# Selecting 32 of 48 keys by dropping the 16 smallest in place of keeping the 32 largest

## The reference

```python
scores = jnp.einsum('bhqd,bhkd->bhqk', q, k) / math.sqrt(D_HEAD)
scores = jnp.where(causal, neg_inf, scores)
vals, idx = jax.lax.top_k(scores, K_S)               # K_S = 32
masked = jnp.put_along_axis(jnp.full_like(scores, -jnp.inf), idx, vals, axis=-1, inplace=False)
attn = jax.nn.softmax(masked, axis=-1)
out = jnp.einsum('bhqk,bhkd->bhqd', attn, v)
...
x = _layernorm(x + attention(x))
x = _layernorm(x + experts(x, ctx_512, itok))
x = _layernorm(x + ffn(x))
```

## Time and profile before

| what | value |
|---|---|
| median of three runs | 606.18 us (605.2 to 607.4) |
| the profiled execution | 605.08 us |
| its span | 603.3 us |
| mean granted clock of TensorE | 0.952 |
| PE busy | 527.5 us (87%) |
| DVE busy | 472.6 us (78%) |
| ACT busy | 385.9 us (64%) |
| POOL busy | 344.5 us (57%) |

### The profile page before, as it was taken

How to read it: one execution, slowest core, us unless ns; L and a number is a source line. 1 busy time by engine, 2 the same in 40 slices (tenths; PEclk the granted TensorE clock), 3 DMA queues, 4 the chain that set the end, 5 groups by cost and what they waited for, 6 DMA issues and landing times. The chain is left out here.

```text
span 603.3 us, 22386 instructions
## 1 busy us (share of the span) xinstructions
PE 527.5 (87%) x8180; PEld 450.2 (75%) x8180; DVE 472.6 (78%) x2995; ACT 385.9 (64%) x909; POOL 344.5 (57%) x336
## 2 busy tenths in 40 slices
PE   4567459999899999998999989998999999989941
PEld 3455347888778878887888878887888888878830
DVE  1777996968988998698899998999899999633213
ACT  2787765866667667675677657776686767555520
POOL 3447661875566646555375646665656556656831
PEclk9799767999999999999999999999999999999985
DMA  7253341010000010000100100010001000000000
GB/s 217 80 184 131 109 145 37 14 37 20 3 21 20 3 54 21 2 3 3 54 20 3 56 3 20 3 55 2 20 3 38 3 3 2 20 0 3 19 0 17
DMA packets 21933, 21.85 MB, mean 36 GB/s; under 512 B 1856, under 2 KB 19776, under 8 KB 21824
## 3 DMA queue, kind: packets, MB, share of 16 engines
q1 hardware_dynamic: 21824, 20.42, 10.8%
HBM read 18.32 MB, written 2.10 MB: 34 GB/s over the span
## 5 line engine op out<-in xcount | busy, mean ns | idle before, releaser
L478 POOL TENSOR_TENSOR h_lo<-h_raw,h_hi 128x512 f16<-128x512 f32 x128 | 148.7, 1164 | 126.8 <-ACT h_raw L598 125.8
L792 PE MATMUL ps_o<-w_hi,h_lo 128*128 128x256 f16 x512 | 139.8, 273 | 4.7 <-POOL h_lo L478 4.5
L776 PE MATMUL ps_z<-x1t_hi,w_lo 128*128 128x256 f16 x512 | 140.4, 274 | 0.7 <-DVE x1t_lo L934 0.7
L776 PE MATMUL ps_z<-x1t_lo,w_hi 128*128 128x256 f16 x512 | 140.2, 274 | 0.0
L776 PE MATMUL ps_z<-x1t_hi,w_hi 128*128 128x256 f16 x512 | 140.1, 274 | 0.0
L792 PE MATMUL ps_o<-w_lo,h_hi 128*128 128x256 f16 x512 | 139.6, 273 | 0.0
L792 PE MATMUL ps_o<-w_hi,h_hi 128*128 128x256 f16 x512 | 139.6, 273 | 0.0
L878 DVE MATCH_REPLACE8 taken<-next,taken 128x48 f32<-128x48 f32 (+2 forms) x576 | 127.4, 232 | 0.1
L594 ACT ACTIVATE h_hi<-ps_z 128x512 f16<-128x512 f32 x128 | 76.0, 594 | 70.5 <-PE ps_z L776 70.4
L499 POOL TENSOR_TENSOR acc<-go_sb,acc 128x512 f32<-128x512 f32 x56 | 71.4, 1276 | 58.9 <-ACT go_sb L608 58.1
L873 DVE MAX8 next<-taken 128x8 f32<-128x48 f32 (+2 forms) x576 | 95.7, 233 | 0.0
(11 more groups left out here) (110 smaller groups left out, 950.3 us busy)
## 6 DMA issues: line engine op xcount, KB each, us to landing
w_raw<-in_w1t SPq DMA_DIRECT2D x8, 512.0 KB, 4.4
w_raw<-in_w2t SPq DMA_DIRECT2D x8, 512.0 KB, 5.5
xt_sb<-in_xt SPq DMA_DIRECT2D x8, 256.0 KB, 3.2
x_sb<-in_x SPq DMA_DIRECT2D x8, 256.0 KB, 2.9
out<-out_sb SPq DMA_DIRECT2D x8, 256.0 KB, 2.2
xa_sb<-in_xt SPq DMA_DIRECT2D x7, 256.0 KB, 3.1
ctx_sb<-in_ctx_w SPq DMA_DIRECT2D x8, 128.0 KB, 2.9
itok_sb<-in_itok SPq DMA_DIRECT2D x8, 128.0 KB, 3.0
```

Of the source, the lines that this page charges most:

```text
L478: nc.gpsimd.tensor_tensor(h_lo[:, e % 2, 2 * z:2 * z + 2, :], h_raw[:, z, :, :], h_hi[:, e % 2, 2 * z:2 * z + 2, :], ALU.subtract)\
L776: last = pe.matmul(ps_z[z][:, d * UT:(d + 1) * UT], w[:, e, c, at:at + P], x[:, c, :], start=n == 0, stop=n == len(terms) - 1)
L792: last = pe.matmul(ps_o[e % 2][:, b * D:(b + 1) * D], h[:, e % 2, c, b * SEQ:(b + 1) * SEQ], w[:, e, c, :], start=n == 0, stop=n == len(te ...
```

## The change

Block 2 has 48 keys, of which 32 stay and 16 go. The 16 that go are now found: ACT writes a second copy of the block's scores, negated and in reversed order, to `s_rev`. Stage 0 finds the 8 largest of it, stage 1 overwrites them into `dropped`, stages 2 and 3 do the same once more, and stages 4 to 6 hold nothing for this block. `keep` becomes two instructions, 48 columns with (dropped read backwards != TAKEN) and 576 columns as before. The reversed order makes equal scores fall as in the reference.

```diff
+DROP = FREE_BLOCKS
+DROPPED = keys(DROP) - TOPK
+DROP_STAGES = 2 * (DROPPED // 8)
+KEEP_FROM = prob_at(DROP + 1)
...
+        s_rev = sb("s_rev", [P, 2, keys(DROP)])
+        dropped = sb("dropped", [P, keys(DROP)])
...
-                    act.activation(s_sb[:, k % 2, :], ps_s[:, LO_FROM:LO_FROM + S_COLS], ACT.Copy).then_inc(s_copied, 1)
+                    act.activation(s_sb[:, k % 2, :], ps_s[:, LO_FROM:LO_FROM + S_COLS], ACT.Copy)
+                    at = LO_FROM + score_at(DROP)
+                    act.activation(s_rev[:, k % 2, ::-1], ps_s[:, at:at + keys(DROP)], ACT.Copy, scale=-1.0)\
+                        .then_inc(s_copied, 1)
...
-                        if r % 2 == 1:
+                        if j == DROP:
+                            s = dropped[:, :] if r > 1 else s_rev[:, k % 2, :]
+                            if r < DROP_STAGES and r % 2 == 0:
+                                last = V.max(next8[:, j, :], s)
+                            elif r < DROP_STAGES:
+                                last = V.match_replace(dropped[:, :], next8[:, j, :], s, TAKEN)
+                        elif r % 2 == 1:
...
-                    V.scalar_tensor_tensor(p_sb[:, k % 2, SEL_FROM:P_COLS], taken[:, SEL_FROM:P_COLS], TAKEN, ps_e,
-                                           ALU.is_equal, ALU.mult).then_inc(p_ready, 1)
+                    V.scalar_tensor_tensor(p_sb[:, k % 2, SEL_FROM:SEL_FROM + keys(DROP)], dropped[:, ::-1], TAKEN,
+                                           ps_e[:, 0:keys(DROP)], ALU.not_equal, ALU.mult)
+                    V.scalar_tensor_tensor(p_sb[:, k % 2, KEEP_FROM:P_COLS], taken[:, KEEP_FROM:P_COLS], TAKEN,
+                                           ps_e[:, KEEP_FROM - SEL_FROM:], ALU.is_equal, ALU.mult).then_inc(p_ready, 1)
```

## The result

The changed kernel takes 603.56 us in the median of 13 runs (601.67 to 604.82), the kernel before 606.56 (13 runs, 604.1 to 607.6). The ratio is 0.9948, 95% interval 0.9934 to 0.9962: 0.5% faster, and more than the 0.3% that can be told from no change. The profiled execution took 602.27 us with a span of 600.5.

The account below looks back on a forecast made before the run. From about 105 us PE was taken as the bound, before that a chain through ACT far more than DVE. The places summed to -1.33 us, 603.75 from the profiled 605.08, 604.8 against the median of 606.18; range 603.0 to 607.3.

Parts of the forecast that it names:

- the first rival: Before 95 us DVE is the limit after all: -0.82 in place of +0.46, sum -2.6, 603.6 us; chance 0.15.
- Per tile: DVE saves 0.46 us and pays 0.05 for the split keep, net 0.41; ACT pays 0.09 for the copy.
- Item 1: Chain to the first expert matmul, before 95 us: four score copies and two keep, no saving that gains, +0.46 us.
- Item 2: At 109.71 us PE waits 0.70 for p_ready; stages 2 to 6 behind DVE's anchor hold all the gain: -0.41 us.
- Item 3: At 160.88 us PE waits 0.64 for x; one whole select and one keep since GpSimd's last lock: -0.41 us.
- Item 4: Tiles at 170, 200 and 265 us: keep stands behind an ACT wait or GpSimd block, +0.05 each, +0.15 us.
- Item 5: turn_x1 at 221.06, 348.99, 411.00, 473.02: savings lost in DVE idle, keep grows, +0.05 each, +0.20; fifth place (286.38) 0.
- Item 6: turn_x2 at 299.79 us: the 0.39 wait vanishes, a whole select standing between anchor and stats: -0.39 us.
- Item 7: Waits of 0.45 for p_sb at 329.33, 391.34 and 453.35 us shrink by 0.31 each, -0.93 us.
- The lock turns over: If keep grows 0.14 us or more, h_lo precedes x, making x 0.20 later four times: 607.3 us; chance 0.15.
- DVE-limited start: DVE limits the kernel before 95 us: two selects and two keep count, -0.82, 603.6 us; chance 0.15.
- The clock: Clock levels before 105 us move with PE's gaps, 1.2 us to either side: 603.6 or 606.0; chance 0.10.

Follow-up runs that it names:

- both_costs: Kernel before with the second reversed score copy on ACT and keep split in two, all seven stages for block 2 kept: ratio 1.0011, median 606.04 us.
- keep_in_four: Changed kernel with keep in four instructions: 607.42 us, ratio 1.0025 to the kernel before.
- x_early_before: Kernel before with the slot of ln1_apply (x) at 40.25 in place of 42, ahead of keep: 607.14 us, ratio 1.0024.
- copy_only: Kernel before with the second, reversed score copy on ACT alone, read by nobody: 606.25 us, ratio 1.0006.
- saving_only: Kernel before with block 2 left out of stages 4 to 6, no second copy, no split keep: 602.85 us, ratio 0.9954.
- split_only: Kernel before with keep split in 48 and 576 columns alone: 606.25 us, ratio 1.0015.
- shift_20: Kernel before with 20 one column memsets of an unused tile on DVE near 4.5 us: 605.55 us, ratio 0.9998.
- shift_64: Kernel before with 64 one column memsets of an unused tile on DVE: 605.92 us, ratio 0.9999.

## Why the prediction was right, and what it missed

The sign of the steady part, the mechanism and the sizes of the single instructions held, and 603.56 lies in the range of 603.0 to 607.3. Its low end was set by the first rival, whose mechanism was not seen, so that the result lies inside is in part luck. I called "within 0.3%" the likeliest at 0.62 and 604.8 as the time, and it came out at 0.5% less: the sum was too small in size, -1.33 us where the profiled executions differ by 2.8 and the medians by 3.0. By its own steps, with the shift of PE's marks between the two profiled executions:

- **Per tile.** Copy 0.09 as forecast, split 0.05 as forecast, 48 wide MAX8 0.12 (219.96 to 220.08 us) against 0.11. The reversed read of `dropped` costs nothing: the small `keep` steps by 0.11 us with it (changed kernel) and 0.10 without it (218.93 to 219.03 in both_costs). The Trainium skill, "VectorE: DVE Perf Modes", section on the TRN2 errata, gave a fixed cost that I turned into estimates of 0.11 for the split and 0.18 for the copy; the rows say half of that.
- **Item 1, before 95 us: forecast +0.46, not found.** The first expert matmul starts at 95.32 us against 95.33. That is two differences that cancel: PE was 0.87 us early at 15 us, where nothing that was changed has run yet (it waited 0.93 in place of 1.88 for `kt_sb` at 14 us), and had lost it by 95. The loss is not the forecast's alone, for between 75 and 90 us the granted clock was 0.50 in place of 0.61. And the start varies between 94.9 and 98.3 us over the 14 traces, so neither +0.46 nor -0.82 (the first rival) is tested by one pair. The times don't tell either: +0.46 us is a ratio of 1.0008, and both_costs, which has all of it, measured 1.0011 (0.9991 to 1.0032). This item stays open.
- **Item 2, 109.71: forecast -0.41, measured -0.70.** The mis-sized term: 0.31 of the wait was the pause of DVE at its number 575. With 128 records less in the trace the number falls on another instruction. I had read "issue" as DVE's work.
- **Item 3, 160.88: forecast -0.41, measured -0.25.** DVE did gain the 0.40 behind its anchor. But the anchor, a block of GpSimd, let one gate sum more stand behind it: it costs 0.21 there, so DVE came out of it 0.56 earlier and PE 0.73.
- **Item 4: forecast +0.15, measured +0.08** (0.61 to 0.62, 0.09 to 0.12, 0.09 to 0.13).
- **Item 5: forecast +0.20, measured +0.15.** 1.46 to 1.51 at three turn_x1; the fourth, at 473, was a wait of 0.39 and stays. The fifth place, forecast 0, gained 0.16 (1.66 to 1.50): in the kernel before a pause (0.22 us, number 1855) had put `x` behind `h_lo`, and now it is ahead.
- **Item 6: forecast -0.39, measured -0.39.**
- **Item 7: forecast 3 x -0.31, measured -0.32, -0.30 and -0.26.**
- **Not counted: the last unit, 0.5 us.** Between 485 and 502 us PE gained 0.47, of which 0.16 is a wait of `scores` at 485.71 that I had left aside as small. The rest I can't name.

Items 2 to 7 sum to -2.15, with the last unit -2.6, of the 2.77 that PE gained behind its first expert matmul. The forecast for the same items was -1.79. So the sum fell short by its first term above all (+0.46, which the pair can neither show nor refute), by what a pause had put on item 2 (0.31, taken for work) and on the fifth place of item 5 (0.16), and by the last unit (0.5), against 0.16 that item 3 did not bring.

The rivals. *The lock turns over* did not happen, at +0.05 of `keep`; in keep_in_four it does, at +0.18, with 1.66 in place of 1.51. I had set the point at 0.14, and the row at 218.47 with 0.09 us left after 0.05 agrees. *DVE-limited start* would have given 603.6, which is what was measured, but the gain lies behind 95 us and not ahead of it, where this rival put it. *The clock* is not ruled out: 7, 5, 7 against 7, 6, 7 in the page's tenths means that between 77 and 81 us the kernel before had 3.4 us at full clock which the changed one had not, and the equal start hides it. From 98 us until PE's last stretch both ran at 1.00. In x_early_before a clock that fell took part.

Also right: DVE's busy time (-11.7, forecast 13), and that most of it does not turn into time (a quarter did, where the forecast had a tenth).

## What to carry to other kernels

Work that is taken from a full but waiting engine is worth what the few waits of the bound engine behind it are worth: go through them one by one, from the anchor of each, and count the small waits too, for here those of the last unit alone made a sixth of the gain. Before a wait is sized, look at whether the releasing engine worked all the time ahead of it; "issue" with nothing to wait for is not work, and moves with any edit. And where a shorter stage leaves slack, look at what can now go earlier: the early `x` lost on the kernel before, and won 2.5 us over the changed kernel once the selection was shorter and the block was moved too.

## What the runs showed of the hardware

**VectorE pauses at numbers of 63 or 64 modulo 128.** The numbers count all of DVE's records in the trace. The pauses take 0.09 to 0.48 us each, three to five are to be seen in an execution, and at the same numbers where DVE's instructions have the same count (575, 1087 and 1855 in the kernel before, in copy_only and in x_early_before). One of the longest, 0.47 us in both_costs, is at number 1983:

```profile
298.30 0.75 DVE L898 SCALAR_TENSOR_TENSOR p_sb<-taken,ps_s 128x576 f32<-128x576 f32 x1
299.52 0.74 DVE L849 TENSOR_SCALAR x<-acc,meanvar,rstd 128x256 f32<-128x256 f32 x2 [0.47 <-issue]
```

They go with the 8 KB packets of the "instruction" queue (above); that they are waits for these is likely and not tested. Nor is it known whether they occur without the profiler. They help to explain why parts did not add up: saving_only and both_costs together would give -2.4 + 0.8, and the change gives -2.3.

**The start comes in steps of 1.8 us.** The same eight matmuls, near 10 us, in the kernel before and in split_only:

```profile
10.15 1.99 PE L654 MATMUL ps_misc<-xt_sb,wk_sb 128*128 128x256 f32 x8 [0.93 <-ACT qt_sb L530]
```

```profile
10.20 3.78 PE L658 MATMUL ps_misc<-xt_sb,wk_sb 128*128 128x256 f32 x8 [0.93 <-ACT qt_sb L534]
```

They take 1.99 or 3.78 us. This is the clock, though the view by stretches prints 1.00 for the granted clock from 10 to 13 us in both. It prints 1.00 too where the trace has no record of the clock, and the first record, of 1.00, comes at 9.04 us in the kernel before and at 14.03 in split_only. Eight matmuls of the same size ahead of both, in the kernel before:

```profile
5.49 3.73 PE L654 MATMUL ps_misc<-xt_sb,wq_sb 128*128 128x256 f32 x8 [5.49 <-DMA wk_sb<-in_wkt]
```

They step by 0.43 us, those at 10.15 by 0.22, and in split_only the matmuls step by 0.43 up to 13 us and by 0.22 from 15 us on. In all 14 traces the step halves where the first clock record stands: at 8.7 to 9.7 us in six, at 13.7 to 14.5 in six, at 18.4 and 18.7 in two. So before that record PE runs at the lower level, 1.2 GHz, and what differs between executions is when it rises.

The same six traces have their first scores at 15.0 to 15.9 us, the other six at 16.6 to 16.9, and the two, where the next eight matmuls are slow as well, at 18.6 and 18.8. By the first expert matmul the 14 traces spread over 3.3 us (94.9 to 98.3), as much as the runs of one kernel do (604.1 to 607.6), and no edit stands ahead of those eight matmuls but DVE's memsets in shift_20 (a fast start) and shift_64 (a slow one).

**A wait can cost more than its length.** 2.18 us of idle PE in the midst of a stretch at full clock were followed by 3 us at 0.50 in one execution, and 2.23 us by none in another.

**The lock works on the first half of a two-part instruction.** `x` for two sequences takes 0.74 us when it starts 0.46 us ahead of `h_lo`, 1.56 when its first half starts ahead of `h_lo` by 0.09 us, and 1.59 when it starts behind by 0.04, in which case PE gets it 0.15 later.
